# A two-layer decoder on one core: the kv and gram steps as a chain of their own, two gram buffers, squares kept in another tile, and new hand-written orders

## The reference, cut to what matters

```python
# layer 0
x = norm(x + mamba(x))                      # W_in, conv of 4 taps, selective scan with 16 states, W_out
kv = ctx @ W_k.T + b_k                      # ctx: (4, 256, 64), the context of a batch
att = softmax(layernorm(scale * (x @ kv) @ kv.T))   # = x @ gram, gram = kv @ kv.T / 16
x = norm(x + att)
x = norm(x + moe(x))                        # 8 experts of 176, top 2, and a shared expert of 352
# layer 1
h = hgrn(x)                                 # h_t = f_t * h_(t-1) + (1 - f_t) * i_t, gate, RMS norm, W_o
x = norm(x + h)
x = norm(2nd mixer)                         # adjacency of the context, top 76 of each row, added to x
x = norm(x + moe(x))                        # 8 experts of 128, top 2, and a shared expert of 256
```

## Time and profile before

| | us |
|---|---|
| median of three executions | 549.06 |
| the profiled execution's own time | 548.52 |
| its span, first to last instruction | 546.6 |
| PE busy in the span | 492.9 |
| DVE busy in the span | 460.6 |
| ACT busy | 369.0 |
| POOL busy | 314.0 |

### The profile page before, as it was taken

One profiled execution on the slowest core, in us unless ns is written; L12 is line 12 of the kernel. 1 busy time (PEld: TensorE's weight loads), 2 busy tenths in 40 slices (PEclk: granted clock), 3 DMA queues, 4 the chain that ended last, 5 costly groups with the idle time before them and its releaser, 6 DMA issues.

```text
span 546.6 us, 10354 instructions
## 1 busy us (share of the span) xinstructions
PE 492.9 (90%) x3266; PEld 429.0 (78%) x3266; DVE 460.6 (84%) x1053; ACT 369.0 (67%) x906; POOL 314.0 (57%) x461
## 2 busy tenths in 40 slices
PE   4868778576889899999999999999999999999996
PEld 3535456344768798999889999898999999999985
DVE  1879969999999999999999999999998778554631
ACT  2599957788799999988877767888894233321110
POOL 0047448954979837859939766677556233232322
PEclk9888766668799999999999999999999999999999
DMA  6130775000066355444243671343446473440000
GB/s 169 23 106 17 245 265 218 19 0 2 4 193 205 112 173 186 126 126 119 67 123 120 212 204 68 110 123 98 153 136 205 129 218 107 135 145 1 11 11 10
DMA packets 26597, 64.16 MB, mean 117 GB/s; under 512 B 4528, under 2 KB 8432, under 8 KB 26160
## 3 DMA queue, kind: packets, MB, share of 16 engines
q1 hardware_dynamic: 26544, 63.50, 37.5%
HBM read 62.38 MB, written 1.11 MB: 116 GB/s over the span
## 4 chain that ended last, share of the span: by engine, by line
PE 53%; POOL 4%; DVE 3%; issue 3%; ACT 2%; POOLq 0%; DVEq 0%; ACTq 0%
PE work L629 32%; PE work L683 13%; PE h_bank L605 4%; PE work L605 2%; POOL dbu L558 2%; DVE acc L1265 1%; ACT dA L1002 1%; POOL hb L580 1%; DVE st L1249 1%; ACT L859 0%; PE work L801 0%; DVE du L1181 0%; DVE row L1079 0%; POOL carry L546 0%; DVE bst L1060 0%
## 5 line engine op out<-in xcount | busy, mean ns | idle before, releaser
L558 POOL TENSOR_TENSOR dbu<-du,b_rows 128x512 f32<-128x512 f32 x128 | 162.8, 1273 | 35.0 <-DMA b_rows<-b_dram 34.2
L1002 ACT ACTIVATE dA<-dts,a_neg 128x127 f32<-128x127 f32 x512 | 156.4, 355 | 20.7 <-DVE st L1249 19.4
L1249 DVE TENSOR_TENSOR_SCAN st<-dA,dbu 128x512 f32<-128x512 f32 x128 | 154.7, 1210 | 3.7 <-ACT dA L1002 1.7
L605 PE MATMUL h_bank<-ident,st 128*128 128x128 f32 x512 | 87.6, 305 | 32.9 <-DVE acc L1265 21.1
L629 PE MATMUL work<-xsT,stream 128*128 128x128 f32 x896 | 109.2, 276 | 0.1
L605 PEld LDWEIGHTS h_bank<-ident,st 128*128 128x128 f32 x512 | 66.3, 157 | 51.9 <-DVE st L1249 41.0
L629 PEld LDWEIGHTS work<-xsT,stream 128*128 128x128 f32 x896 | 104.7, 192 | 2.0 <-issue 1.2
L1265 DVE SCALAR_TENSOR_TENSOR acc<-h_bank,c_cols,acc 128x512 f32<-128x512 f32 x128 | 92.9, 726 | 6.4 <-PE h_bank L605 6.2
L580 POOL TENSOR_TENSOR hb<-hb,wbt 128x512 f32<-128x512 f32 (+2 forms) x48 | 54.4, 1141 | 39.9 <-ACT wbt L859 19.9
L508 POOL TENSOR_SCALAR var<-mv 128x1 f32<-128x1 f32 x56 | 13.5, 241 | 71.2 <-DVE mv L1065 70.8
L683 PE MATMUL work<-stream,hb 128*128 128x256 f32 x224 | 53.0, 380 | 0.1
(11 more groups left out here) (156 smaller groups left out, 767.6 us busy)
## 6 DMA issues: line engine op xcount, KB each, us to landing
stream<-in_stream SPq DMA_DIRECT2D x48, 512.0 KB, 4.0
stream<-in_stream SPq DMA_DIRECT2D x48, 384.0 KB, 3.5
b_rows<-b_dram SPq DMA_DIRECT2D x32, 256.0 KB, 4.9
wg<-in_wg SPq DMA_DIRECT2D x1, 1280.0 KB, 7.6
wu<-in_wu SPq DMA_DIRECT2D x1, 1280.0 KB, 10.2
wd<-in_wd SPq DMA_DIRECT2D x1, 1280.0 KB, 12.8
xT<-in_xT SPq DMA_DIRECT2D x4, 256.0 KB, 3.6
out<-row SPq DMA_DIRECT2D x8, 128.0 KB, 2.1
```

The lines of the kernel that those rows point to most:

```text
L558: gp.tensor_tensor(tile, du[:, batch % 2, :, lo:hi], b_rows[:, q % B_RING, at:at + 1, :].to_broadcast([P, ET, P]), ALU.mult).then_inc(s["d ...
L605: return nc.tensor.transpose(dst, src, ident[:, :])
L1002: last = A(dA[i % DA_RING][:, t, 1:P], dts[:, batch % 2, t, lo + 1:hi], ACT.Exp, scale=a_neg[:, t, k:k + 1])
L1249: V.tensor_tensor_scan(st[:, i % ST_RING].rearrange("p t l -> p (t l)"), dA[i % DA_RING].rearrange("p t l -> p (t l)"), dbu[:, i % DBU_RIN ...
```

## The change

1. A chain `k` of its own: `("kv", b, 0)` makes `kv` and `("kv", b, 1)` makes `gram` of batch b. `out` 0 and `out` 1 keep their places in chain `m` and have nothing to do on PE and ACT.
2. `gram` has two buffers (b % 2). ACT waits for the gram product of the batch before ahead of overwriting `kv`, and for the last `att` product of batch b-2 ahead of overwriting its `gram` buffer.
3. `sq` is no tile of its own: the squares are written to `tf`. ACT waits for `ss` of the unit before ahead of writing `tf`.
4. All five orders and the deal of banks are new; every step stays on its engine.

```diff
@@ chains
+        "k": [("kv", b, k) for b in range(B) for k in range(2)],
@@ ORDER, first four lines of PE's and DVE's, first two of ACT's, POOL's first, SP's
     "pe": [
-        "ppaaaeppppppespesssssesppssspemsssssaaaaaaaaaaaaamsasapppsssssssssmmsmspsssssssssssssessssppmmmmsmpsssssmmmmmm",
-        "mmmmmmmfssmfsssffffffffsfssmmmmssmfmmmmmmmmmmffsssesffsfsmssffsmmsfsfpppsmffffpffhsshshffffffffssfffsmmmmsshhh",
-        "hmfffssssfpppfssffsgmmmmmmmmmmmmmsgffffmsgfhhhhhhhhhfshfffffffsshggggggfsmmmmggmshhhhsfgfsffssfssgmmmmmmmmmmff",
-        "fssssggsgsaaaaaaaaaaaaafasfmsggggmmaggmffffgggggghhhhhhhhhgsghgsgshfggsfssfffffffgfeffsfhhhhsfsfsmmmmssffmffgg",
...
+        "ppaaaepppsepppepsssssesskppspssssspppsssskpsssaaaaaaaaaaaaassssmmmmssssssssssasassmesssppssssmmmmksmsspsessksm",
+        "mmmmmmmmmmmmsmsskffssffffffffssfssmmmmmfffesssffssfsssfssfsfpppsmmmmmmmmmmmmmssfmffffpffsfffffffshhsfsmmmmhmss",
+        "fffhhhhssssfsppfssffssfpfsfffffmmmmmmmmmmmmmssgmsggsfggggghhhhhhhhhsghssfhgsssgmmmmgfffffffmfssshhhhsgffsgsffs",
+        "sggsfffsfaaaaaaaaaaaaafkassggggfaggmmmmmmmmmmmmmgggggsmshhhhhhhhhghffffgsfhfsfffffffsfffgfgfshhhhssgffmmmmfmff",
...
     "dve": [
-        "ppaaaaaaaaaappppppsssssspsassssasaassassasssaaasassssssssssssssmmmmmssssmsppppppmssssmpssassmmmmammssmmmmssmss",
-        "ssmmmmmsmffmssffsmafsfmmfmfffmsssmsmffsmsmsmmfffssssfffasssffffmmmmmmmfmppppppfffspsffsfmffhhhhfhfssfahhsffmmh",
-        "mmssssfffhhsmsfffahmhhmhmsmmhsmffffsfggggmmmmmfsffmssamsffmfafgghhhhgfgfahffssmmhhmmggshssmmffhsfffhammsssshsm",
-        "hhgggfffmshsssgggshagfffgmfsgggfggaaagafgmmmmmaaggasaggsgggssffsmsgggmffaffhhhhffhffaffshhsghhmhsfffhghahshamm",
...
+        "ppaaaaaaaaaapppppssspsssspsasssassassssassassssassssssssssssssppppppspsmmmmmaaamamssssmsssssmmmsmmmsmmmmssmsss",
+        "mmmmmsmffsmffsasamfsfafmmfmfmsssfsamffmsfffsssmmssmfffmssasssafffmfmmmmmfsmfmffpppppppsffsmsfafsfmmfhhhhffhffs",
+        "ssmsmhhsshmfffmhsmshmssmhmhfffhshamsfffhfsfsggmmmmmsmggfffasggmssmgffsfgshhhhfhfggfsssmmfmfmshhshgggmhsffhsmsh",
+        "shfffhhasssggghgammgmfffsmsffffaaafagggggfggamggmmmmmasassmffaggfffffmfffhhhhffmhssafffhhaggghshhassshahmmafff",
...
     "act": [
-        "ppaapaespppsppsssspssepeesspsspssaaaaaaaaaaasmsppsaaasasssssssssmsmmssssssssssppsssssssepsspmmmmmsspmmmsspsssm",
+        "ppaapaespppspspspsssssepeespssspssssksppsssaaaaaaaaaaasssssssmmmmssssssskssaaaspssspaepsssspsmmmmmskssspmmmsss",
...
     "pool": [
-        "ssssssssssssssssspppppppppppppsssssssmmmsssssssssssspssssssssssmmsssssmmmmmsmmmmmsmmmmmmmsssssssssssmmppppppsh",
+        "sssssssssssssssssssssssspppppppppppppsssmmmssspssssssssssssssssmmssssssmmmmmmmmmmmmmmmmmsssssssssssssmmsmmmmmh",
...
     "sp": [
-        "llllllbxrrcrblrcrrcrrrrclrrxrccrcrccrbwccrccccwcccccwrcccrcrccccrccrccccrcbcorrccrccrrcrrwcccccccccorcccrccccc",
-        "wcccocccccwccccccccccccocccccccccccccocccccooo",
+        "llllllbrcrxlrrrbrccrrrrrrrlcbrcwxcrrcccccrrrrcccrcwccccccccccccwwrrrbccccccrccrcccccorccrcccccccccocrwccrccrcc",
+        "ccorwcccccccccccccccccoccccccccccccccocccccooo",
@@ decoder
-        gram = sb("gram", [P, LT, L])
+        gram = sb("gram", [P, 2, LT, L])
-        sq = sb("sq", [P, HT, P])
+        sq = tf
@@ PE
-                if stage == "out" and k == 0:
-                    batch, lt = divmod(b, LT)
+                if stage == "kv" and k == 0:
...
-                    if lt == 0:
-                        t = claim("kv", b)
-                        fill(mm(t[0:C, 0:L], wkvT[:, :], ctxT[:, batch], start=True, stop=True), "kv", b)
+                    t = claim("kv", b)
+                    fill(mm(t[0:C, 0:L], wkvT[:, :], ctxT[:, b], start=True, stop=True), "kv", b)
-                if stage == "out" and k == 1 and b % LT == 0:
+                if stage == "kv" and k == 1:
                     pe.wait_ge(*read("kv", b))
                     t = claim("gram", b)
...
                     if b % LT == 0:
-                        pe.wait_ge(*read("gram", b))
+                        pe.wait_ge(*read("gram", b // LT))
                     t = claim("att", b)
-                    fill(product(t, 0, lambda c: xsT[MIX0][:, c, :], lambda c: gram[:, c, :], LT, L), "att", b)
+                    fill(product(t, 0, lambda c: xsT[MIX0][:, c, :], lambda c: gram[:, b // LT % 2, c, :], LT, L), "att", b)
@@ ACT
-                if stage == "out" and k == 0:
-                    if b % LT == 0:
-                        evacuate("kv", b, kv[:, :], work_bank("kv", b)[0:C, 0:L], func=ACT.Identity, bias=b_k[:, :])
+                if stage == "kv" and k == 0:
+                    if b:
+                        act.wait_ge(*full("gram", b - 1))
+                    evacuate("kv", b, kv[:, :], work_bank("kv", b)[0:C, 0:L], func=ACT.Identity, bias=b_k[:, :])
...
-                if stage == "out" and k == 1 and b % LT == 0:
-                    evacuate("gram", b, flat(gram[:, :, :]), scale=1.0 / 16)
+                if stage == "kv" and k == 1:
+                    if b >= 2:
+                        act.wait_ge(*full("att", LT * (b - 1) - 1))
+                    evacuate("gram", b, flat(gram[:, b % 2]), scale=1.0 / 16)
...
                 if stage == "hgrn" and k == 2:
+                    if b:
+                        act.wait_ge(*full("ss", b - 1))
                     evacuate("hf", b, flat(tf[:, :, :]), work_bank("hf", b)[:, 0:HT * P], func=ACT.Tanh, scale=0.5)
```

More of the change, by code:

```diff
@@ L111 @@
+        "mmmffffhhhhfmfhhhhhhhhhffffffffhfmmmmffmggggfgghffggggggfffggfgffffhhhhggfgfghhhhhhhhhfffffffffffggggfhffghffa",
+        "aaaaaaaaaaaaffghhhhgggggggghhhhhhhhhghhgggggggghhhhggggggggggggggggggggggggggggggggggppsmmmmmmmmmfffhhhhhhhhgg",
+        "g",
     ],
     "dve": [
-        "ppaaaaaaaaaappppppsssssspsassssasaassassasssaaasassssssssssssssmmmmmssssmsppppppmssssmpssassmmmmammssmmmmssmss",
-        "ssmmmmmsmffmssffsmafsfmmfmfffmsssmsmffsmsmsmmfffssssfffasssffffmmmmmmmfmppppppfffspsffsfmffhhhhfhfssfahhsffmmh",
@@ new lines @@
+        "ssmmfffffsmhhfggghsmgsgsgmggmmmggssgghhhhggamhggsmmmmmmffgggmassmhhshhaaaffffhffffssffsfffashshmmhmhhsssfffsms",
+        "gggsmgfffgffmsgggfgggmmmggmsgmmmmssggmmffsmffmfsmfffsffsffhhhhmmsfffammhagggmsmssfffgggmmmmssmmmmggffffhhffhhh",
+        "ffmmgmfffmfamhhffffhahhammffmmfffmmggggmmgggmmhhhhaaahfffgamggffffhhgggfhhfhhffffaffgggffhhhhfgfgffgffffffhhhh",
+        "ahggggggfffhffhfhhgghgghhhhggghhhhhhhggggghggghggggghhhhhhghggggggggggggggggggggggggggggggpppppeeeeeeeekkkkkkk",
+        "k",
@@ new lines @@
+        "mmmmmmmmmmmkssssffskssspefffffffffsmmmmmssffssfmmmssssfffsssssmmmmmmmmmmmseppffffffffpfsshpsssfhffffffffmmmmmh",
+        "sshhhhsffssfsmmmsspsfffsspsmmmmmmmmmmmffffffffsgspsgfshhhhhhhhhsgggggggssshfhggmmmmmsshhhhssgffffffffssffssaaa",
+        "aaaaaaaafsssfffmmmssaaaskggggggggasmmmmmmmmmmmgghhhhhhhhhpgggggghffffffffshfsfffffffffffhhhhfggsssgsssmmmmmfff",
+        "ssaaaaaaaaaaasshhhhhhhhhksmmmggggggggehshssggggggggmmmmmmmmmmmgghhhhffffffffgssfsaaaasmmmmmsfffffffffsfffsssff",
+        "fsssssggggggggssmmmsgggggggghhhhhhhhhskmmmmmmmmmmmsffffffffsggfshfffffffffmmmmmshssfffgshhhhsmmmfffmmmmmmmmmmm",
@@ new lines @@
+        "gggggggggmmggshhhshsgggsssssssfffffffffffffffhhhmmmmmfffsfffsssgggfffmmmmmssssgggggggggggmmmmmmmmmggssffffffff",
+        "fffffffssmmmmmfffshhhhhhhhgggfffmmmmmgggfffhhhmmmmmmmmmhhhhmmmmmffffffffffffffffffhhhhhhhhfffmmmmmgggggggggggh",
+        "hhggfffhggghhhgggfffffffffffffffffffffhhhhhhhhhhhfffhggggggggggghhhgggggggghhhhhhhhhhhhhhhgggggggggggggggggggg",
+        "ggggggggggggggggggssaaaaaaaaaaaaaaaaaaaaaaaaaaaaaaaaaaaaaaaaaaaaaaaaaaaaaaaaaaaaammmmeeeeeeeekkkkkkkkfffhhhhgg",
+        "g",
@@ L163 @@
     ("adj", "w"): ["wqk"], ("adj", 0): ["qk"], ("adj", 1): ["sim"], ("adj", ROUNDS + 4): ["adjT"],
-    ("gate", 0): ["gate"], ("out", 3): ["yT"], ("out", 4): ["mamba"],
+    ("gate", 0): ["gate"], ("kv", 0): ["kv"], ("kv", 1): ["gram"], ("out", 3): ["yT"], ("out", 4): ["mamba"],
     ("xat0", 0): ["x1T"], ("xat0", 1): ["att"],
@@ L178, in banks @@
 def banks(stage, i, k):
-    first = {0: ["kv"], 1: ["gram"]}.get(k, []) if stage == "out" and i % LT == 0 else []
-    return first + BANKS.get((stage, k), [])
+    return BANKS.get((stage, k), [])
 MIX0, FFN0, MIX1, FFN1 = range(4)
```

37 lines of the change are left out of this document (11 added, 26 removed).

## The result

The changed kernel takes 550.91 us (median of 14 executions, 549.06 to 553.18) against 549.31 of the kernel before (14 executions on the same chip, 548.15 to 551.17). The ratio is 1.0036 with a 95% interval of 1.0021 to 1.0050: slower, by some 2 us (0.36% of 549). The forecast had the sign and three and a half times the size: 6.9 us.

The account below looks back on a forecast made before the run. DVE was taken to set the pace from 80 to 200 us, PE full from 200 on. 548.5 + 6.9 (unit 4's turn) + 0 (early gaps) = 555.4 us, range 544.5 to 561.

Parts of the forecast that it names:

- part 4: DVE's early waiting: worked sum +1.2 us, bounds -5.9 (both gaps go, nothing new) to +2.9, taken as 0.
- Start, +2.3: At unit 0's start, POOL's second state waits for both units' dts, with 2.4 us of convolution still to do: +2.3 us.
- The gap behind `pre` (2, 1), +2.4: pre(2,1) takes the place just ahead of unit 0's last turn, so DVE gets a new gap: +2.4 us.
- The wait for unit 1's first dA, +2.3: Two adjacency rounds that filled DVE's wait for unit 1's first dA are gone from there: +2.3 us.
- The table loads: Five fewer ACT table loads ahead of unit 4's scan, 6.4 us of ACT; gain at most -1.7 us through DVE's dA waits.
- the gap of 4.15: DVE's largest early gap, for unit 0's last turns behind pre(2,0), goes because that product moves ahead: -4.15 us.
- Part 3: Orders at three turns: unit 3 +3.6, unit 4 +6.9 (15.6 more PE work left, 8.7 earlier), unit 5 +3.7; largest decides.
- Parts 1 and 2: Chain k, the second gram buffer and the squares in tf, with ACT's new waits: gain 0, cost 0.
- A (faster): Rival: early gaps close (-5.9), only unit 3's +3.6 holds, small reorderings give 1.5: 544.7 us; chance 0.22.
- C: Rival, more waits: work banks held longer by batch 2's hid0 and hid1, five handovers cost DVE +5: 560.4 us; chance 0.12.
- D: Rival, the clock: PE's low clock level lasts 5 us longer, 2.5 us more: 557.9 us; chance 0.06.
- marks for "wrong": DVE idle before 200 us falls over 4 us, PE idle after exceeds 2, or unit 3's last turn comes over 4 earlier.

Follow-up runs that it names:

- e9_mirror114: Changed code, order of the kernel before up to 114 us, then the change's: 560.80 us, ratio 1.0221; with the cut at 155 us: 562.39 us, 1.0245.
- e1: The changed code with the orders and banks of the kernel before: 548.68 us, ratio 0.9993 to the kernel before.
- e8: The changed kernel with DVE's first scan of unit 5 moved behind the routing and first weighting of ffn0 unit 2: 551.41 us, ratio 1.0039.
- e5: Changed code, the change's order up to 112 us, then that of the kernel before, banks dealt anew: 548.92 us, ratio 0.9991.
- e6: Changed code, the change's order up to 150 us, then that of the kernel before, banks dealt anew: 547.28 us, ratio 0.9956.
- e11: Orders of e6, but from about 265 us on the bank pattern of the kernel before: 545.10 us, ratio 0.9939 to the kernel before.
- e4: The changed kernel with pre(2,0) put back on PE directly ahead of the turn of unit 0's state 14: 552.81 us, ratio 1.0067.

## Why the prediction was wrong in size

**The sum, with what was measured.** Everything is counted from the first load (PE's first product at 6.1 us before, 7.1 in the change, 6.1 in the mirror), profile against profile, at the turn of unit 4's state 14:

| against before, us | forecast | change | `e9_mirror114` |
|---|---|---|---|
| DVE's busy time up to its sum | -6.8 | -8.4 | -8.7 |
| DVE's idle time up to there | 0 | -4.3 | +2.9 |
| PE behind DVE's sum (1.9 before) | -1.9 | -1.8 | -1.8 |
| PE begins the turn | -8.7 | -14.5 | -7.7 |
| left behind it | +15.6 | +18.2 | +19.9, of it 1.7 banks |
| sum | +6.9 | +3.7 | +12.2, without the banks +10.5 |

(A tenth may be lost by rounding.) The spans of the two profiles differ by 4.7 us: 3.7 and the 1.0 of the later load. The medians give +1.6, the ratio +2.0. The 2.1 between 3.7 and 1.6 is how the two profiles lie to their medians: the change's 1.3 over its own, without that load, and the one before 0.8 under. So a single profile is good to some 2 us here. With e1's profile for before (DVE idle 12.6 us up to this sum, in place of 14.8) and e8's for the change (9.0, in place of 10.5; its one move lies behind this turn), the -4.3 is anything from -2.1 to -5.8. The sign holds in every pairing.

**The step that failed is part 4, "I take 0".** The step put DVE's waiting at no change, from a worked sum of gains and losses; DVE waits 4.3 us less (2.1 to 5.8, as above), toward the lower bound (-5.9). With -4.3 in its place the forecast would have been +2.6 us, slower by 0.5%. The three losses that I had added did not come:
- *Start, +2.3.* I had POOL, and so unit 0's second state, wait for the dts of both units, made behind the first scan, and then for the taps of the convolution. The string has seven `p` steps of DVE ahead of the first scan, which make both; only the eighth is moved behind it. Timeline after:

```profile
35.17 1.64 DVE L1208 TENSOR_TENSOR du<-dts,hs 128x512 f32<-128x512 f32 x1
...
36.76 1.22 DVE L1256 TENSOR_TENSOR_SCAN st<-dA,dbu 128x512 f32<-128x512 f32 x1
37.03 3.72 POOL L562 TENSOR_TENSOR dbu<-du,b_rows 128x512 f32<-128x512 f32 x3
...
37.90 2.40 DVE L1188 SCALAR_TENSOR_TENSOR du<-work,cw,du 128x255 f32<-128x255 f32 x6
```

  The 2.40 us of taps run while POOL makes input terms, and up to its sum ahead of unit 0's state 14 DVE is idle as long as before (6.2 and 6.3 us). (The mark "unit 0's second state no earlier than 38 us" was met, at 40.22, and so proves little.)
- *The gap behind `pre` (2, 1), +2.4.* DVE's idle time there became 1.02 us, and it was for `sim` from ACT. I had in mind the 3.78 us of the neighbour, at the lower level of the clock; this one ran 1.99.
- *The wait for unit 1's first dA, +2.3.* It is 0.32 at 77.19, and DVE's waits for dA up to the turn grew from 1.4 to 2.8 us in all.

The table loads, the one gain that I had booked, gave none. There are five fewer ahead of unit 4's turn, as listed (29 and 34), and 21 before dA in the whole kernel where there were 27, and DVE still waits more for dA.

```profile
L1004 ACT ACT_TABLE_LOAD x21 | 26.9, 1283 | 0.4
```

The Trainium skill (ScalarE: Activation LUTs, What ACT_TABLE_LOAD costs) has a drain of about 1380 ns at each switch. ACT's idle time before these 21 loads is 0.4 us in all, so here too none of it shows as idle time.

What went is DVE's waiting for the turns of PE, 5.7 us before and 0.3 after: not only the gap of 4.15 whose cause was moved, but nearly all. The prediction names that ("each of them can shrink a little") and then lets losses cancel it that did not come.

**Part 3 had the right turn and the right form, with two sizes off.** What is left at units 5 and 7 is what the lists of steps said, to 0.5 us. At unit 4, 2.6 us more are left. From that turn to the end (window, us, PE busy), before and after:

```profile
255.54:546.60 291.06, 284.05 (x2101) 1.00 0.38 116
```

```profile
242.04:551.30 309.26, 300.65 (x2236) 1.00 0.39 118
```

PE's busy time behind the turn is 16.6 us more where the lists gave 15.6, and its idle time is 1.6 more (8.6 and 7.0) where the sum took it to be the same. e8 shows that moving one step does not take that idle time away. On the other side DVE's busy time up to its sum is 8.4 us less, and I had counted 6.8. The two errors nearly cancel (+2.6 - 1.6), which is luck. At unit 3 the lists were worse: 8.5 us more are left, not 4.0, by 5.9 of PE's busy time (342.9 and 337.0) and 2.6 of its idle time; where the other 1.9 of busy time comes from I did not find.

At unit 5 the forecast had +3.7, and the profiles, without the load, differ by 3.7 too. That is luck as well: PE is tied to DVE there, DVE's busy time up to that sum is 0.5 us less (286.9 and 287.4) and not 3.6, and its idle time is 2.7 less and not the same. From unit 4's turn to unit 5's DVE's busy time grew by 4.7 us more than the lists have, which fits the longer instructions told of above (4.4 us in all).

**What the mirror adds.** Without the early part, the late order costs 10.5 us by profile, and by medians 1.0221 x 549.0 - 549.0 - 1.7 = 10.4. 2.9 of it is what its DVE waits more than before, about the wait of its join; with DVE's waits as before, which is what the forecast's turn sum supposed, 7.6 are left, near its 6.9. That is the best support for part 3. The mirror's DVE waits 7.2 us more than that of the change, and 4.4 of this (12.1 and 7.7 up to the sum ahead of unit 1's state 15) lies ahead of the join.

**Parts 1 and 2**, at nothing, are shown right by e1.

**The rivals.** A (faster) asked for 5.2 us less waiting and for no more than +3.6 at the turns. It had 3.5 us of the first by 200 us and 4.3 by the turn, and the kernel is slower all the same, since the turn of unit 4 decides as forecast. C is not what happened: DVE's waits for PE fell. D neither: the granted clock from 80 to 200 us is 0.86, it was 0.83. Of the marks for "wrong", PE's idle time behind 200 us over 2 us was met (3.8), and unit 4's turn does leave more than the sum had; unit 3's last turn came 3.8 us earlier, where 4 was the mark, and DVE's idle time up to there fell from 13.2 to 9.7 us, by 3.5, where 4 was.

**What the early order is worth.** Early and late order together make the time:

| | late order of before | late order of the change |
|---|---|---|
| early order of before | 0.9993 (e1) | 1.0221, 1.0245 (e9) |
| early order of the change | 0.9991 (e5), 0.9956 (e6), 0.9939 (e11) | 1.0036 |

With 0.3% off e5, e6 and e9 for their banks, the early order seems to be worth 1.5 to 1.8% in the right column (8.5 to 9.8 us) and 0.3 to 0.7% in the left (1.8 to 3.7 us). The joins make most of that difference. In the right column they make the kernel without the early order slower, by 2.5 to 3.9 us of DVE's waits (e9); in the left they take from the kernel with it: from the sum ahead of one unit's state 15 to that of the next, DVE is idle 4.7 us behind the join of e5 (1.4 and 1.9 in the two kernels, units 1 to 2), 1.4 behind that of e6 and 1.6 behind that of e11 (0.4 and 0.1, units 2 to 3). An estimate from these numbers is 6 us in the right column and 4 to 5 in the left; with intervals of 1 to 2 us to each side of every ratio, a difference between the columns is not shown.

Nor is a slack of PE seen to swallow the early gain. In e5, e6 and e11 PE begins the turn of unit 4 2.0 us behind DVE's sum, as before, and that of unit 3 0.6 us behind, as before: with the late order of before the handover is at unit 3's end, and what is left behind it stays at 343.7 us in e11, 344.0 before.

## What to carry to other kernels

Where two engines hand the limit to each other, look for the moment of the handover: the time is when the first engine reaches it plus what the second has left, and both must be counted from the lists of steps. Waits of the first engine ahead of the handover go into the first part, so a forecast must book them one by one, not leave them at zero between two bounds. An early and a late half of a new order should each be tried with the other half of the old one: here the change hides a gain of half a per cent behind a loss that is larger. But a join has waits of its own, 2.5 to 4.3 us for the largest here, as much as the effect looked for; read them from the profile of the joined kernel before its time is taken for the worth of a half.

## What the runs showed of the hardware

- The same orders repeat themselves to 0.1 us from unit 3 on (what is left at four turns, before and e1) and differ by 2.6 us ahead of unit 1, the first load's landing (5.9 to 7.1 us in all profiles) not counted.
- The eight instructions of an in-projection took 3.62 and 1.99 us within six microseconds in e4, at granted clocks of 0.50 (1.2 GHz, from 69.1 to 72.5 us) and 1.00 (2.4 GHz, from 74.5 to 76.3). Before the change the same product as the first of these took 3.78 us and in the change the second took 1.99. A price read in such a part of one profile has the clock of its moment in it.
- Which banks the same products write to, in an unchanged order, made a difference of 1.7 us in a stretch that PE fills, from unit 7's last turn to the end (126.4 us in e6, 124.7 in e11).
- DVE's product of two SBUF tiles (L1208) took 0.69 us alone, at 33.84 us, and 1.64 us at 35.17, beside POOL's product of two SBUF tiles from 34.68 to 36.27. The Trainium skill (SBUF — State Buffer, SBUF: two separate sides) has DVE, with two SBUF inputs, and a GpSimd operation that reads SBUF exclude each other, so that the one that comes second waits for the first to end. Here DVE's ended 0.54 us after POOL's did, less than its own 0.69, so it was not held wholly; and the scans of DVE run beside the same POOL instruction at 1.21 to 1.22 us all through the kernel (36.76 above).
